# Second masks left out for one source tile in eight of a masked graph attention layer: their sums made on TensorE as adjacency times values minus first mask times values

## The reference

```python
A_tilde = A + eye(N); mask = A_tilde > 0
Wh = (x @ W.T).reshape(N, 4, 32)
score_l, score_r = einsum('nhd,hd->nh', Wh, a_l), einsum('nhd,hd->nh', Wh, a_r)
e = score_l[:, :, None] + score_r.T[None, :, :]
e = where(e >= 0, e, 0.2 * e)
e = where(mask[:, None, :], e, -inf)
alpha = softmax(e, axis=2)
out = elu(einsum('nhm,mhd->nhd', alpha, Wh).reshape(N, 128))
return layernorm(x + out)
```

## Time and profile before

| | |
|---|---|
| median of 3 runs | 1857.82 us |
| profiled execution | 1858.71 us |
| its span, first to last instruction | 1856.8 us |
| VectorE (DVE) busy | 1789.7 us, 96% |
| ScalarE (ACT) busy | 1723.1 us, 93% |
| TensorE (PE) busy | 1655.9 us, 89% |
| mean granted TensorE clock | 0.969 |
| moved by DMA | 420.05 MB |

### The profile page before, as it was taken

How to read it: one execution, slowest core, us unless ns; L and a number is a source line. 1 busy time by engine, 2 the same in 40 slices (tenths; PEclk the granted TensorE clock), 3 DMA queues, 4 the chain that set the end, 5 groups by cost and what they waited for, 6 DMA issues and landing times.

```text
span 1856.8 us, 81511 instructions
## 1 busy us (share of the span) xinstructions
PE 1655.9 (89%) x37063; PEld 1622.3 (87%) x37063; DVE 1789.7 (96%) x2120; ACT 1723.1 (93%) x1855; POOL 42.5 (2%) x26
## 2 busy tenths in 40 slices
PE   6088899899999989899998999999998999989895
PEld 5088899798998989899997989989898989989895
DVE  5689999999999999999999999999999999999997
ACT  4599899899998999999998999999999999989994
POOL 1000000100000000010001000010000100010000
PEclk8598999999999999999999999999999999999998
DMA  6989777686766767676776867667777767666221
GB/s 218 352 291 347 242 228 257 212 266 224 246 207 222 260 218 244 218 248 218 233 240 214 267 217 249 212 234 245 229 233 234 251 200 263 216 219 209 58 73 35
DMA packets 240408, 420.05 MB, mean 226 GB/s; under 512 B 14400, under 2 KB 104896, under 8 KB 238016
## 3 DMA queue, kind: packets, MB, share of 16 engines
q1 hardware_dynamic: 240064, 414.83, 68.2%
HBM read 397.48 MB, written 17.30 MB: 223 GB/s over the span
## 4 chain that ended last, share of the span: by engine, by line
issue 80%; PE 5%; DMA 5%; ACT 4%; DVE 4%; POOL 2%; SPq 1%; POOLq 0%; DVEq 0%; ACTq 0%
ACT bmask L393 3%; DMA abuf<-in_adj_dram 3%; PE psum L316 3%; POOL vrs L711 1%; PE psum L270 1%; DMA v_scratch<-vt 1%; DVE bmask L561 1%; DMA vring<-v_scratch 1%; DVE bmask L549 1%; DVE cmask L567 0%; PE psum L279 0%; POOL vrs L708 0%; PE trp L303 0%; DVE acc L573 0%; DVE vt L503 0%
## 5 line engine op out<-in xcount | busy, mean ns | idle before, releaser
L393 ACT ACTIVATE bmask<-lrow,rtab 128x1024 fp8e4<-128x1024 f32 x1450 | 1545.5, 1151 | 45.3 <-PE psum L316 44.5
L316 PE MATMUL psum<-vring,bmask 128*128 128x99 bf16 x16384 | 829.6, 208 | 95.5 <-DVE bmask L561 46.5
L316 PEld LDWEIGHTS psum<-vring,bmask 128*128 128x128 fp8e4 x16384 | 765.8, 98 | 111.7 <-issue 81.3
L316 PE MATMUL psum<-vring,cmask 128*128 128x99 bf16 x16384 | 832.2, 209 | 24.3 <-DVE cmask L567 16.7
L316 PEld LDWEIGHTS psum<-vring,cmask 128*128 128x128 fp8e4 x16384 | 765.2, 98 | 35.9 <-DVE cmask L567 27.9
L561 DVE TENSOR_TENSOR bmask<-bmask,acache 128x1024 int32<-128x1024 int32 x512 | 624.1, 1219 | 12.3 <-ACT bmask L393 9.1
L567 DVE TENSOR_TENSOR cmask<-acache,bmask 128x1024 int32<-128x1024 int32 x512 | 623.8, 1218 | 11.0 <-PE psum L316 11.0
L549 DVE TENSOR_SCALAR bmask<-lrow,rtab 128x1024 fp8e4<-128x1024 f32 x598 | 439.7, 747 | 0.0
L303 PE MATMUL trp<-pack,abuf 128*128 128x32 bf16 x4096 | 143.4, 177 | 49.3 <-ACT acache L361 35.1
L303 PEld LDWEIGHTS trp<-pack,abuf 128*128 128x128 bf16 x4096 | 127.0, 97 | 53.8 <-issue 19.9
L361 ACT CAST acache<-trp 128x512 int32<-128x512 f32 x256 | 148.2, 579 | 12.3 <-PE trp L303 12.3
(11 more groups left out here) (59 smaller groups left out, 201.8 us busy)
## 6 DMA issues: line engine op xcount, KB each, us to landing
abuf<-in_adj_dram SPq DMA_DIRECT2D x256, 1024.0 KB, 8.1
vring<-v_scratch SPq DMA_DIRECT2D x512, 198.0 KB, 3.7
lrow<-l_scratch SPq DMA_DIRECT2D x16, 1024.0 KB, 11.0
v_scratch<-vt SPq DMA_DIRECT2D x16, 792.0 KB, 10.2
bmask<-in_x_dram SPq DMA_DIRECT2D x16, 256.0 KB, 3.0
late<-in_x_dram SPq DMA_DIRECT2D x32, 128.0 KB, 5.1
out_dram<-late SPq DMA_DIRECT2D x32, 128.0 KB, 6.4
l_scratch<-cmask SPq DMA_DIRECT2D x1, 128.0 KB, 3.7
```

Source lines behind the costliest of these rows:

```text
L316: return nc.tensor.matmul(psum[:, bank, at * S3:(at + 1) * S3], mask[:, i, j * P:(j + 1) * P], vring[:, q % 4, i, col:col + S3], start=ope ...
L393: last = nc.scalar.activation(bmask[:, q % 4, h, i], lrow[:, p, h], ACT.Relu, bias=rtab[:, t, H + hh:H + hh + 1], scale=BIG, saturate=False)
```

## The change

In every fourth step (q % 4 == 3) the second tile (i = 1) gets no second mask. Its second sums are made from the turned adjacency tile times the second values of both heads in one product of 198 columns, and from the first mask times the negated second values, which are added in the same PSUM words. For this:

- `mask_c` works on one tile in those steps, 512 words instead of 1,024.
- TensorE makes, in those steps, 8 products of 198 columns with adjacency as weights and 16 of 99 columns with the first mask, ahead of the turned pair and after `half_done`; of the products with the second mask 16 are left.
- Each table of values gets 198 more columns, the negated ones, made by a new `negate` on VectorE; `store_v` waits for it (`v_neg`) where it waited for `v_lo`, and stores 3,366 columns instead of 3,168. Every fourth `load_v` takes 990 columns instead of 792.
- The order of items in PSUM is sub-block by sub-block, so that two heads lie side by side, and banks hold 5, 5, 5, 5, 4, 4, 4 items instead of 5 in six and 2 in the last.
- `evacuate` waits for `mm_done` instead of `c_ready` where the tile it overwrites was read by such a product.

```diff
+    def by_sum(q):
+        return q % (G // 2) == G // 2 - 1
...
-                sp.wait_ge(v_lo, n + 1)
-                sp.dma_start(v_dram[p, :, G * g:G * g + G], vt[:, n % VS].rearrange("q t i e -> q t (i e)")).then_inc(v_out[n % VS], 16)
+                sp.wait_ge(v_neg, n + 1)
+                sp.dma_start(v_dram[p, :, g], vt[:, n % VS]).then_inc(v_out[n % VS], 16)
...
                 last.then_inc(half_done, 1)
+                if by_sum(q):
+                    at = (c * NT + 2 * s + 1) % RING
+                    for j in range(SUB):
+                        product(acache[:, at], 1, j, 0, 1, NW, heads=HP)
+                        for h in range(HP):
+                            product(bmask[:, q % 4, h, 1], 1, j, h, 1, VW + h * S3)
                 for r in TURNED[q]:
                     turn_pair(r)
                 pe.wait_ge(c_ready, q + 1)
-                for i in range(2):
...
+                for i in range(1 if by_sum(q) else 2):
...
-                    act.wait_ge(c_ready, step_no(before // STEPS, 1, before % STEPS) + 1)
+                    step = step_no(before // STEPS, 1, before % STEPS)
+                    act.wait_ge(mm_done if by_sum(step) else c_ready, step + 1)
...
+            def negate(n):
+
+                dve.wait_ge(v_lo, n + 1)
+                nc.vector.tensor_scalar(vt[:, n % VS, G * VW:GW], vt[:, n % VS, G * VW - NW:G * VW], -1.0, None, ALU.mult).then_inc(v_neg, 1)
...
                 rest(g)
+                if g > 1:
+                    negate(g - 2)
                 if g > 0:
                     lowest(g - 1)
+            negate(NG - 2)
             lowest(NG - 1)
...
+                tiles = 1 if by_sum(q) else 2
+                nc.vector.tensor_tensor(mask_words(cmask[:, q % 2], tiles), adj_words(c, s, tiles), mask_words(bmask[:, q % 4], tiles),
                                         ALU.bitwise_xor).then_inc(c_ready, 1)
```

More of the change, by code:

```diff
@@ L25, in gat_kernel @@
     PB = 512 // S3
-    BANKS = -(-ITEMS // PB)
     FIRST_BANKS = HP * SUB // PB
+    IN_BANK = [PB] * (FIRST_BANKS + 1) + [PB - 1] * 3
+    BANKS = len(IN_BANK)
+    START = [sum(IN_BANK[:b]) for b in range(BANKS)]
+    PLACE = [(b, k) for b in range(BANKS) for k in range(IN_BANK[b])]
     VW = HP * 2 * S3
+    NW = HP * S3
     WH = H * E + 2 * H
@@ L62, in on_scalar @@
         return 3 if q % 6 else 2
+    def by_sum(q):
+        return q % (G // 2) == G // 2 - 1
+    GW = G * VW + NW
+    assert len(PLACE) == ITEMS and G // 2 == 4
     COMPARES = [(i, h) for i in range(2) for h in range(HP)]
@@ L161, in wait, with table, ring @@
                 eng.wait_ge(s, value)
+        def table(n):
+            return vt[:, n % VS, 0:G * VW].rearrange("p (i w) -> p i w", w=S3)
+        def ring(q, i, col, width):
+            at = (q % 4 * 2 + i) * VW + col
+            return vring[:, at:at + width]
         @block.sync
@@ L308, in step, with product @@
                 w = c * NP + p
-                def product(mask, item, i, h, b, j):
-                    bank, at = item // PB, item % PB
+                def product(mask, i, j, h, b, col, heads=1):
+                    item = (b * SUB + j) * HP + h
+                    bank, at = PLACE[item]
                     opening = s == 0 and i == 0 and at == 0
@@ L314, in product @@
                         wait(pe, bank_free, BANKS * (w - 1) + bank + 1)
-                    col = (h * 2 + b) * S3
-                    return nc.tensor.matmul(psum[:, bank, at * S3:(at + 1) * S3], mask[:, i, j * P:(j + 1) * P],
-                                            vring[:, q % 4, i, col:col + S3], start=opening, stop=True, skip_group_check=True)
+                    return nc.tensor.matmul(psum[:, bank, at * S3:(at + heads) * S3], mask[:, j * P:(j + 1) * P],
+                                            ring(q, i, col, heads * S3), start=opening, stop=True, skip_group_check=True)
                 pe.wait_ge(v_in[q % 4], 16 * (q // 4 + 1))
@@ L321, in step @@
                 for i in range(2):
-                    for h in range(HP):
-                        for j in range(SUB):
-                            last = product(bmask[:, q % 4, h], h * SUB + j, i, h, 0, j)
+                    for j in range(SUB):
+                        for h in range(HP):
+                            last = product(bmask[:, q % 4, h, i], i, j, h, 0, h * S3)
                 last.then_inc(half_done, 1)
+                if by_sum(q):
+                    at = (c * NT + 2 * s + 1) % RING
+                    for j in range(SUB):
+                        product(acache[:, at], 1, j, 0, 1, NW, heads=HP)
+                        for h in range(HP):
+                            product(bmask[:, q % 4, h, 1], 1, j, h, 1, VW + h * S3)
                 for r in TURNED[q]:
@@ L328, in step @@
                 pe.wait_ge(c_ready, q + 1)
-                for i in range(2):
-                    for h in range(HP):
-                        for j in range(SUB):
-                            last = product(cmask[:, q % 2, h], (HP + h) * SUB + j, i, h, 1, j)
+                for i in range(1 if by_sum(q) else 2):
+                    for j in range(SUB):
+                        for h in range(HP):
+                            last = product(cmask[:, q % 2, h, i], i, j, h, 1, NW + h * S3)
                 last.then_inc(mm_done, 1)
@@ L411, in _ @@
             for b in range(2):
-                nc.scalar.activation(uu[:, :, b], um[:, b], ACT.Exp).then_inc(uu_done, 1)
+                for p in range(NP):
+                    nc.scalar.activation(uu[:, :, b, p], um[:, b, :, p * HP:(p + 1) * HP].rearrange("q c h j -> q c j h"),
+                                         ACT.Exp).then_inc(uu_done, 1)
             compare(0)
@@ L492, in rest @@
                 k = n % 2 if n < NG else 2
-                dst = vt[:, n % VS].rearrange("p t i e -> p (t i) e")
+                dst = table(n)
                 dve.wait_ge(v_hi, n + 1)
@@ L516, in _ @@
             nc.vector.tensor_tensor(tl, l_rows, top, ALU.add).then_inc(tl_done, 1)
+            negate(NG - 1)
             dve.wait_ge(tl_done, 1)
@@ L522, in words, with adj_words, mask_words @@
                 return ap.bitcast(i32)
[L524 removed]
+            def adj_words(c, s, tiles=2):
                 at = (c * NT + 2 * s) % RING
[L526 to L530 removed]
+                pair = words(acache[:, at:at + tiles].rearrange("p t n -> p (t n)"))
+                return pair.rearrange("p (o n) -> p o n", o=1).to_broadcast([P, HP, tiles * CI // 4])
+            def mask_words(mask, tiles=2):
+                return words(mask[:, :, 0:tiles].rearrange("p h i n -> p h (i n)"))
             def add_diagonal(c, half):
@@ L658, in _ @@
                         lowest(NG + q // EVERY_STEPS - 1)
+                        negate(NG + q // EVERY_STEPS - 1)
                     if q < STEPS:
```

44 lines of the change are left out of this document (20 added, 24 removed).

## The result

The changed kernel takes 1897.97 us (median of 4 runs, 1896.49 to 1898.45) against 1858.8 us for the kernel before (4 runs, 1857.31 to 1861.83): a ratio of 1.0207, 95% interval 1.019 to 1.0225. It is slower by 39 us, where 28 were forecast. Its span is 1896.0 us against 1856.8.

The account below looks back on a forecast made before the run. VectorE was taken to bound sweeps before the change, TensorE with waits from VectorE's place after it. 1858.7 + 14 (start) + 2 (bytes) + 14 (sweeps) - 4 (last sweep) + 4 (clock) = 1888.7, median 1887 us; range 1858 to 1914.

Parts of the forecast that it names:

- rival 1: Sweeps: VectorE stays the bound and TensorE's added 5.5 us fit into its waits; about 1810 us, chance 0.02.
- rival 3: Sweeps: ScalarE's masks come late when VectorE has caught up, 2 us more a sweep; 1925 us, chance 0.12.
- 534 ns a step: VectorE's xor in 128 steps falls from 1,024 to 512 words; 4.3 us a sweep, 68 us in all.
- TensorE's added products: Steps by sum: eight products of 198 columns at 86 ns each, 0.69 us a step, 5.5 us a sweep.
- Sixteen products merely change weights: TensorE, steps by sum: sixteen products only take other weights; the added time is that of eight 198-column products.
- TensorE's sweep without waits becomes 103.7 us: TensorE's own work in a sweep, 98.2 us before, with 5.5 us of added products.
- The waits: Sweep's start: TensorE waits for VectorE, 2.8 us, or 6.6 after every second sweep; mean 4.7.
- The forecast sweep: Inner sweeps: TensorE's 103.7 plus 4.7 us of waits, 108.4 against 107.35; +14 us over fourteen.
- the bounds that I list: Range of the total: start -6 and +6, waits +-1.2 us a sweep (17 in fourteen), clock -4 and +11.
- The start: Ahead of the main loop: each table store waits for the last one's landing, +14 us; more bytes, +2.
- Clock: Sweeps: TensorE's stretches at the lower clock level, formerly hidden by VectorE's lateness, come onto the path; +4 us.
- The last sweep's -4: Last sweep, without turned pairs: VectorE bound it before and keeps its saving of 4.3 us; -4 us.

Follow-up runs that it names:

- e2: Against e1, VectorE makes the whole xor of 1,024 words in every step again, TensorE's work being that of the change: 1901.4 us.
- e3: Against e1, half xor kept but TensorE makes 64 plain products, so second sums are not the reference's: 1848.47 us.
- e4: Against e1, no step by sum; the changed order of items and products and the larger tables stay: 1866.23 us.
- e10: Against e1, plain products go head by head with sub-blocks inside, as before the change; places in PSUM stay: 1875.9 us.
- e5: Against e1, VectorE's work at a sweep's start spread over later steps, ScalarE's and SyncE's following parts moved later too: 1873.21 us.
- e12: Against e5, SyncE's output store and residual load in step 24 instead of 26, VectorE's and ScalarE's late parts one to three steps earlier: 1867.7 us.
- e1: Against the changed kernel, each table's negate stands right behind its own lowest, so stores no longer wait for the previous landing: 1886.31 us.

## Why the prediction was right, and where it was off

**What bounds the kernel.** VectorE before, TensorE with waits brought in by VectorE's place in the sweep after: right. The bank reads wait 28.3 us where they waited 2.1, VectorE is idle 12.0 us in 64 steps (12 foretold), and the fast rival 1 (1810 us) fell: in e2 VectorE's whole saving is worth 15 us, and in e3, where nothing is paid for it, the kernel still takes 1848. Of rival 3, the three-way coupling, there is a trace: VectorE's waits for ScalarE's comparisons rose from 9.1 to 20.5 us. How much of TensorE's waits comes from them was not tried.

**VectorE.** 534 ns a step foretold, 535 measured; `negate` takes 0.21 us in the timeline, for 0.2.

**TensorE's added products.** The eight groups of a wide product and its two narrow ones take 1156.18 - 1154.77 = 1.41 us, 0.176 each. Less two of 44.8 ns that leaves 87 ns, for 86 foretold. This term was right. The Trainium skill's N / 2.4 + 2.5 ("TensorE: Matmul & The Clock Gate", section "Back-to-back issue gap") gives 85 for 198 columns; this trace agrees with it within 2 ns.

**The step that was off** is "Sixteen products merely change weights", and with it "TensorE's sweep without waits becomes 103.7 us". It is 104.7: the prediction took the new order of all other products (for each sub-block the two heads in turn, instead of all sub-blocks of one head and then of the other) to be free. It costs 0.13 us in four steps, over both kinds of phase. e4 shows it without sums, and e10 takes it away and lands on 12.96 us for four steps. 1.0 us a sweep more is 15 us over fourteen sweeps by count and 10 to 12 as measured (e10).

**The waits.** 2.8 and 6.6 us a sweep were foretold, 4.7 in the mean. Sweeps of 108.04 and 111.31 us, less 104.7, give 3.3 and 6.6; the idle times of the weight loads in these two sum to 3.0 and 6.0. Over twelve sweeps the mean is 1319.6 / 12 - 104.7 = 5.3. The mechanism and its size held. e5, which only moves work, takes away 30 us of the waits for first masks, so the work at a sweep's start, VectorE's above all, is their cause (some of ScalarE's and SyncE's moved with it). It is not shown for all of the 5.3 us: with the work spread a sweep still takes 109.1 (e5) or 108.3 us (e12), 3.6 or more above 104.7.

**Luck in the sum.** The forecast sweep was short by more than the missing 11 us show: 109.97 where 108.4 was foretold, 1.0 of it by TensorE's own work and 0.6 by the waits. Against this the kernel before takes 1295.2 / 12 = 107.93 a sweep, and not the 107.35 of the one window that I read. Over fourteen sweeps I had the kernel after 22 us too short and the kernel before 8 us too short, and in the difference the one takes from the other. Also, the bounds that I list add up to 1860 to 1921 and not to 1858 to 1914; the result lies in both.

**The start.** 14 + 2 us foretold, 11.5 + 2.3 measured, of which e1 gives back 11.7. Most landings were shorter (4.57 to 5.64 us) than the 5.28 and more that I took.

**Clock and last sweep.** The clock cost nothing that shows: six windows of about two sweeps each have a grant of 1.00 where before they had 0.99, so those 4 us were wrong. The last sweep's -4 did not come either: from the seventh mark to the end the kernel is 1.1 us slower. The first offsets the second. Why the last sweep kept nothing was not tried.

## What to carry to other kernels

Here three engines within a few per cent of each other, with rings of two to four buffers between them, took 2 to 5 us a sweep (2 to 5%) more than the fullest of them had work. Relieving the one that looked full bought little (18 of 64 us), while loading the one behind it cost more than that (38 us, for 8 x 0.69 x 15 = 83 us of products). And read more than one window: the pair of sweeps on which the forecast was built was the shortest of six. Before such an exchange, count the distance from every engine to the next, and look where a wait, here the end-of-sweep read, throws away an engine's lead. A bookkeeping step put behind an unrelated one in an in-order queue (a negation behind the next table's `rest`) can chain transfers that were free of each other, and this was the cheapest 12 us to win back.

## What was not expected of the hardware

- The order in which the same products are issued changes their rate: 32 products of 99 columns take 1.45 us with the heads in turn and 1.43 with the sub-blocks inside (the changed kernel against e10), in the phases of first and of second masks alike; behind a turned pair it is 1.42 against 1.41.
- With eight DMA issues of SyncE in step 24 instead of 26, and VectorE's and ScalarE's late parts one to three steps earlier, the waits for values were 16.5 instead of 27.0 us (e12 against e5). Which of these moves did it was not separated.
